# Last feed-forward unit by tile, two residuals on ScalarE and Pool, last output in two stores

## The reference, cut to what matters

```
x = x + xattn(ctx, layernorm(x), mask)
h = silu(q(n) @ q(w_gate).T) * (q(n) @ q(w_up).T)     # n = layernorm(x), 352 columns
x = x + q(h) @ q(w_down).T
```

## Time and profile before

| what | value |
|---|---|
| median of 3 runs | 218.21 us (218.11 to 219.34) |
| profiled execution | 219.57 us, span 217.6 us, so 1.97 us lie outside the span |
| TensorE busy | 187.8 us, 86% |
| VectorE busy | 176.5 us, 81% |
| Pool busy | 139.3 us, 64% |
| ScalarE busy | 131.8 us, 61% |
| granted TensorE clock, mean of the run | 0.973 |

### The profile page before, as it was taken

One profiled execution on the slowest core, in us unless ns is written; L12 is line 12 of the kernel. 1 busy time (PEld: TensorE's weight loads), 2 busy tenths in 40 slices (PEclk: granted clock), 3 DMA queues, 4 the chain that ended last, 5 costly groups with the idle time before them and its releaser, 6 DMA issues.

```text
span 217.6 us, 5689 instructions
## 1 busy us (share of the span) xinstructions
PE 187.8 (86%) x2045; PEld 141.5 (65%) x2045; DVE 176.5 (81%) x391; ACT 131.8 (61%) x264; POOL 139.3 (64%) x203
## 2 busy tenths in 40 slices
PE   0839988979998999998998998796898988899963
PEld 0318574856967769587696775475676766677753
DVE  6417785898799876978769987999999999999941
ACT  2362697957878877798786744364455383665441
POOL 6272737188969592672926577676689875777750
PEclk9985999999999999999999999699999999999998
DMA  6999632040200000000000000000101010101111
GB/s 190 268 293 345 225 115 81 7 144 3 96 3 5 3 0 0 5 3 3 0 3 5 0 5 0 0 0 2 50 3 48 0 48 3 48 2 51 48 49 48
DMA packets 13665, 11.97 MB, mean 55 GB/s; under 512 B 766, under 2 KB 10558, under 8 KB 13630
## 3 DMA queue, kind: packets, MB, share of 16 engines
q1 hardware_dynamic: 13078, 11.29, 16.8%
q10 hardware_dynamic: 560, 0.33, 0.5%
HBM read 9.52 MB, written 2.10 MB: 53 GB/s over the span
## 4 chain that ended last, share of the span: by engine, by line
PE 31%; POOL 20%; issue 14%; DVE 7%; ACT 4%; POOLq 0%; DVEq 0%; ACTq 0%
POOL hq L372 7%; POOL wq_y L357 5%; PE bank L890 4%; PE bank L946 4%; PE bank L949 3%; PE bank L899 3%; PE bank L900 2%; PE bank L878 2%; PE bank L970 2%; POOL xn L254 2%; ACT xn L411 2%; PE a_pair L841 2%; POOL sch L364 2%; PE bank L841 2%; ACT val L423 2%
## 5 line engine op out<-in xcount | busy, mean ns | idle before, releaser
L970 PE MATMUL bank<-wdT,hT 128*128 128x128 f32 x192 | 27.1, 278 | 4.1 <-issue 3.3
L946 PE MATMUL bank<-guT,xqT 128*128 128x352 f32 x64 | 25.5, 481 | 4.3 <-DVE hh L732 4.3
L372 POOL TENSOR_TENSOR hq<-wq_u,sch 128x704 f32<-128x704 f32 x16 | 22.6, 1410 | 9.5 <-DVE wq_u L759 9.4
L970 PEld LDWEIGHTS bank<-wdT,hT 128*128 128x128 f32 x192 | 23.9, 191 | 5.4 <-issue 4.4
L949 PE MATMUL bank<-guT,xqT 128*128 128x352 f32 x64 | 25.0, 473 | 0.0
L357 POOL TENSOR_TENSOR wq_y<-hh,ivh 128x704 f32<-128x704 f32 x16 | 22.5, 1407 | 3.9 <-DVE ivh L747 3.3
L878 PE MATMUL bank<-cT,wsT 128*128 128x512 f32 x32 | 16.9, 655 | 6.5 <-DMA cT<-in_ctxT 6.5
L477 ACT ACTIVATE mask_bc<-bank 128x352 f32<-128x352 f32 x32 | 14.7, 458 | 12.3 <-PE bank L946 12.3
L545 ACT COPY hT<-bank 128x384 f32<-128x384 f32 x32 | 15.2, 476 | 10.2 <-PE bank L958 10.2
L532 ACT ACTIVATE a_pair<-wq_y 128x704 f32<-128x704 f32 x16 | 12.2, 763 | 14.8 <-DVE wq_u L759 14.4
L612 DVE TENSOR_REDUCE den<-prob 128x8 f32<-128x512 f32 x32 | 19.8, 666 | 0.0
(11 more groups left out here) (117 smaller groups left out, 497.2 us busy)
## 6 DMA issues: line engine op xcount, KB each, us to landing
cT<-in_ctxT SPq DMA_DIRECT2D x8, 512.0 KB, 5.2
x_all<-in_x SPq DMA_DIRECT2D x8, 256.0 KB, 5.5
mask_bc<-in_mask_rows SPq DMA_DIRECT2D x8, 256.0 KB, 6.3
out_y<-mask_bc SPq DMA_DIRECT2D x8, 256.0 KB, 2.2
wsT<-in_WsT ACTq DMA_DIRECT2D x1, 256.0 KB, 4.2
w_all<-in_wg SPq DMA_DIRECT2D x1, 176.0 KB
w_all<-in_wu SPq DMA_DIRECT2D x1, 176.0 KB
w_all<-in_wd SPq DMA_DIRECT2D x1, 176.0 KB
```

The lines of the kernel that those rows point to most:

```text
L372: nc.gpsimd.tensor_tensor(hq[i][:, :, 0:I].rearrange("p t (n k) -> p t n k", k=BLK), rh[i][:, :, :].rearrange("p (t n) k -> p t n k", t=2) ...
L946: nc.tensor.matmul(gu_bank[2 * n % 3][:, 0:I], xqT[g % 2][:, t], guT[:, 0, :], start=True, stop=True).then_inc(pe_g, 1)
L970: last = nc.tensor.matmul(d_bank[:, j * P:(j + 1) * P], hT[n % 2][:, c, :], wdT[:, c, :], start=(c == 0), stop=(c == 2))
```

## The change

Unit 15, the last, is handled by tile from the scaled product on. Pool computes `yh` in two instructions (`y_tile`), ScalarE takes the absolute values in two (`abs_tile`), each into a bank of its own that the gate and up products no longer use, and VectorE rounds in four (`round_tile`), and so none of them waits for `ah`. The product with the scale is done by Pool for tile 30 (`hq_first_tile`) and by VectorE for tile 31 (`hq_last_tile`). The groups 5 and 6 (`D_BY_ACT`) are read out of `d_bank` by ScalarE (`down_evac`, a plain copy to `y_out`), and Pool adds `x_all` in place (`residual_sum`), both after `hq_first_tile`. The down products of group 7 go to two other banks, tiles 28 to 30 in one, tile 31 in the other. VectorE adds them to `x_all` in two parts (`residual_last`), three tiles and one, and SyncE stores these as two DMAs. `yo_ok` becomes one semaphore per group.

```diff
+LAST_U = UNITS - 1
+D_BY_ACT = (NG - 3, NG - 2)
...
+        at_bank, last_d = (w1, av_bank), (w0, w0, w0, banks[2])
...
+            def store_last(part, t):
+                sp.wait_ge(yo_ok[NG - 1], part)
+                sp.dma_start(out_tiles[:, NT - TILES + t.start:NT - TILES + t.stop, :],
+                             y_out[1][:, t, :]).then_inc(out_d[1], 16)
...
-            for g in range(NG):
+            for g in range(NG - 1):
                 store(g)
+            store_last(1, slice(0, TILES - 1))
+            store_last(2, slice(TILES - 1, TILES))
...
+            def y_tile(t):
+                pool.wait_ge(ivh_ok, UNITS)
+                pool.wait_ge(h_ok, NT)
+                pool.wait_ge(rh_ok, LAST_U - 1)
+                b = slice(t * NB_H, (t + 1) * NB_H)
+                nc.gpsimd.tensor_tensor(yh[1][:, b, :], hh[1][:, b, :],
+                                        ivh[1][:, b].unsqueeze(2).to_broadcast([P, NB_H, BLK]), ALU.mult).then_inc(yt_ok, 1)
+
+            def hq_first_tile():
+                pool.wait_ge(rt_ok, 1)
+                pool.wait_ge(sch_ok, UNITS)
+                pool.wait_ge(pe_t, t_place["h", NT - 5] + 1)
+                nc.gpsimd.tensor_tensor(hq[1][:, 0, 0:I].rearrange("p (n k) -> p n k", k=BLK), rh[1][:, 0:NB_H, :],
+                                        sch[LAST_U % 4][:, 0:NB_H].unsqueeze(2).to_broadcast([P, NB_H, BLK]),
+                                        ALU.mult).then_inc(hqt_ok[0], 1)
+
+            def residual_sum(g):
+                pool.wait_ge(d_ok, D_BY_ACT.index(g) + 1)
+                ys = y_out[g % 2][:, :, :]
+                nc.gpsimd.tensor_tensor(ys, ys, x_all[:, tiles(g), :], ALU.add).then_inc(yo_ok[g], 1)
...
-                if 0 <= u - 2:
+                if 0 <= u - 2 < LAST_U:
                     hq_unit(u - 2)
...
+                if u < LAST_U:
                     y_unit(u)
+                if u == LAST_U:
+                    y_tile(0)
+                    y_tile(1)
+                if u == UNITS + 1:
+                    hq_first_tile()
+                    residual_sum(D_BY_ACT[0])
+                    residual_sum(D_BY_ACT[1])
...
+            def abs_tile(t):
+                act.wait_ge(yt_ok, t + 1)
+                act.wait_ge(h_ok, NT)
+                nc.scalar.activation(at_bank[t][:, 0:I], yh[1][:, t * NB_H:(t + 1) * NB_H, :].rearrange("p n k -> p (n k)"),
+                                     ACT.Abs, scale=MAGIC).then_inc(at_ok, 1)
+
+            def down_evac(g):
+                act.wait_ge(pe_dn, (g + 1) * TILES)
+                past(act, out_d[g % 2], 16 * (g // 2))
+                nc.scalar.copy(y_out[g % 2][:, :, :].rearrange("p t d -> p (t d)"), d_bank[:, :]).then_inc(d_ok, 1)
+
             for m in range(NT + LAG + 1):
+                if m >= NT and (m - LAG - 1) % TILES == 0 and (m - LAG - 1) // TILES - 1 in D_BY_ACT:
+                    down_evac((m - LAG - 1) // TILES - 1)
...
-                if m % 2 and 0 <= (m - 3) // 2 < UNITS:
+                if m % 2 and 0 <= (m - 3) // 2 < LAST_U:
                     h_abs((m - 3) // 2)
+                if m == 2 * LAST_U + 3:
+                    abs_tile(0)
+                    abs_tile(1)
...
+            def residual_last(t):
+                dve.wait_ge(pe_dn, NT - TILES + t.stop)
+                dve.wait_ge(out_d[1], 16 * (NG // 2 - 1))
+                nc.vector.tensor_tensor(y_out[1][:, t, :],
+                                        last_d[t.start][:, t.start * D:t.stop * D].rearrange("p (t d) -> p t d", d=D),
+                                        x_all[:, NT - TILES + t.start:NT - TILES + t.stop, :],
+                                        ALU.add).then_inc(yo_ok[NG - 1], 1)
+
+            def round_tile(t):
...
+                nc.vector.scalar_tensor_tensor(out=uh[:, t, :], in0=at_bank[t][:, 0:I], scalar=FLOOR * MAGIC,
+                                               in1=yh[1][:, b, :].rearrange("p n k -> p (n k)"),
+                                               op0=ALU.max, op1=ALU.add).then_inc(ut_ok, 1)
...
+                nc.vector.scalar_tensor_tensor(out=rh[1][:, b, :].rearrange("p n k -> p (n k)"), in0=at_bank[t][:, 0:I],
+                                               scalar=FLOOR * MAGIC, in1=uh[:, t, :],
+                                               op0=ALU.max, op1=ALU.subtract).then_inc(rt_ok, 1)
+
+            def hq_last_tile():
...
+                nc.vector.tensor_tensor(hq[1][:, 1, 0:I].rearrange("p (n k) -> p n k", k=BLK), rh[1][:, NB_H:, :],
+                                        sch[LAST_U % 4][:, NB_H:].unsqueeze(2).to_broadcast([P, NB_H, BLK]),
+                                        ALU.mult).then_inc(hqt_ok[1], 1)
 
             for m in range(NT + LAG + 2):
                 if m < NT:
                     h_product(m)
-                if m < NT and (m - LAG) % TILES == 0 and on((m - LAG) // TILES - 1):
+                if (m - LAG) % TILES == 0 and 0 <= (m - LAG) // TILES - 1 < D_BY_ACT[0]:
                     residual((m - LAG) // TILES - 1)
...
+                if m == 2 * LAST_U + 4:
+                    round_tile(0)
+                    round_tile(1)
+                    hq_last_tile()
...
-                if m >= NT and (m - LAG) % TILES == 0 and on((m - LAG) // TILES - 1):
-                    residual((m - LAG) // TILES - 1)
+            residual_last(slice(0, TILES - 1))
+            residual_last(slice(TILES - 1, TILES))
...
             def h_transpose(n):
-                pe.wait_ge(hq_ok, u + 1)
+                if u < LAST_U:
+                    pe.wait_ge(hq_ok, u + 1)
+                else:
+                    pe.wait_ge(hqt_ok[n % 2], 1)
...
             def down(n):
+                bank = d_bank if g < NG - 1 else last_d[j]
+                if n == NT - 1:
+                    pe.wait_ge(rh_ok, LAST_U)
                 if j == 0:
-                    past(pe, yo_ok, g)
+                    if g == NG - 1:
+                        pe.wait_ge(h_ok, NT)
+                    elif g - 1 in D_BY_ACT:
+                        pe.wait_ge(d_ok, 1)
+                    elif g > 0:
+                        pe.wait_ge(yo_ok[g - 1], 1)
```

More of the change, by code:

```diff
@@ L160, in xattn_ffn @@
             sem(n) for n in ("pe_x0", "x0_ok", "pe_t", "t_ok", "pe_g", "pe_u", "pe_dn"))
-        sg_ok, h_ok, amh_ok, uph_ok, ivh_ok, sch_ok, yh_ok, ah_ok, uh_ok, rh_ok, hq_ok, yo_ok = (
+        sg_ok, h_ok, amh_ok, uph_ok, ivh_ok, sch_ok, yh_ok, ah_ok, uh_ok, rh_ok, hq_ok, d_ok = (
             sem(n) for n in ("sg_ok", "h_ok", "amh_ok", "uph_ok", "ivh_ok", "sch_ok", "yh_ok", "ah_ok",
-                             "uh_ok", "rh_ok", "hq_ok", "yo_ok"))
+                             "uh_ok", "rh_ok", "hq_ok", "d_ok"))
+        yt_ok, at_ok, ut_ok, rt_ok = (sem(n) for n in ("yt_ok", "at_ok", "ut_ok", "rt_ok"))
+        hqt_ok = [sem(f"hqt_ok{t}") for t in range(2)]
+        yo_ok = [sem(f"yo_ok{g}") for g in range(NG)]
         x_tiles = x.rearrange("(n p) d -> p n d", p=P)
@@ L193, in store @@
             def store(g):
-                sp.wait_ge(yo_ok, g + 1)
+                sp.wait_ge(yo_ok[g], 1)
                 sp.dma_start(out_tiles[:, tiles(g), :], y_out[g % 2][:, :, :]).then_inc(out_d[g % 2], 16)
+            def store_last(part, t):
+                sp.wait_ge(yo_ok[NG - 1], part)
+                sp.dma_start(out_tiles[:, NT - TILES + t.start:NT - TILES + t.stop, :],
+                             y_out[1][:, t, :]).then_inc(out_d[1], 16)
             load_x(0)
@@ L221, in _ @@
                 load_c(g)
-            for g in range(NG):
+            for g in range(NG - 1):
                 store(g)
-            for s in range(2):
-                sp.wait_ge(out_d[s], 16 * (NG // 2))
+            store_last(1, slice(0, TILES - 1))
+            store_last(2, slice(TILES - 1, TILES))
+            sp.wait_ge(out_d[0], 16 * (NG // 2))
+            sp.wait_ge(out_d[1], 16 * (NG // 2 + 1))
         @block.gpsimd
@@ L775, in _ @@
                     s3_round(NG - 3)
-                if m % 2 == 0 and 0 <= m // 2 - 2 < UNITS:
+                if m % 2 == 0 and 0 <= m // 2 - 2 < LAST_U:
                     h_round(m // 2 - 2)
+                if m == 2 * LAST_U + 4:
+                    round_tile(0)
+                    round_tile(1)
+                    hq_last_tile()
                 if m % 2 and m < NT:
@@ L969, in down @@
                 for c in range(3):
-                    last = nc.tensor.matmul(d_bank[:, j * P:(j + 1) * P], hT[n % 2][:, c, :], wdT[:, c, :],
+                    last = nc.tensor.matmul(bank[:, j * P:(j + 1) * P], hT[n % 2][:, c, :], wdT[:, c, :],
                                             start=(c == 0), stop=(c == 2))
```

11 lines of the change are left out of this document (10 added, 1 removed).

## The result

The changed kernel took **217.50 us** (median of 7, 217.08 to 217.67), the kernel before 218.78 (median of 7, 218.11 to 219.65). The ratio is 0.9935, with a 95% interval of 0.9912 to 0.9959: shorter by 0.65%. That is less than the 1% which the prediction took as the least that can be told from no change. Forecast were 216.3 and a range of 215.8 to 217.0, a gain of 1.89 us. The median missed the range by 0.5 us, and the gain came out 0.5 to 0.6 smaller.

A forecast was written before the change was run, and what follows sets the result against it. No one engine sets the span; in the tail VectorE sets T28. Gains of 0.48 and 0.74 us up to D31's end, then earlier residual and stores, make 1.89 saved: 218.21 - 1.89 = 216.3 us, range 215.8 to 217.0.

The forecast's parts named there:

- the sum's own time: Whole kernel: the 1.89 us saved in the tail, taken off the median of three, 218.21, gives 216.3.
- The residual of group 5: VectorE after product 31: moving this residual to ScalarE and Pool starts tile 28's transposes 0.48 us earlier.
- T28: TensorE's three transposes of tile 28's quantised product: would start at 207.92 us, 0.48 earlier than 208.40.
- The banks: TensorE, down matmuls of tiles 28 to 31: two banks nobody has to empty remove a wait, 0.74 us in all.
- D31's end: End of tile 31's three down matmuls, TensorE's last work: 212.98 us forecast, against 214.20 before.
- ScalarE's copy of group 6: New ScalarE copy before tile 29's down matmuls: just fits, costed at nothing, with 0.1 us as its other end.
- The second store's quarter: Last group's second store: its quarter of the traffic ends before the stream would, so the end is first issue + 2.2 us.
- Rival 1: Last residual: nothing holds it, as Pool's sum goes ahead of VectorE or is nearer 1.06; 2.18 us saved, 216.0, chance 0.2.
- 0.1 to either side: Margin in us kept for the added semaphores, which have no row; the nearest existing waits cost under 0.1 each.
- The split's weight: Unit 15 by tile: makes room for the banks' gain, since tile 30's transposes would otherwise wait until 211.04 us.
- Rival 3: Store of group 5 lands 0.5 us later still, through a slower sum or T28 less early: 216.8, chance 0.12.
- Rivals 2 and 4: 2: last group's second store pays its whole latency, 216.7, chance 0.13; 4: TensorE's clock falls from T28, 221.4, chance 0.04.

The follow-up runs named there:

- a5_unit_whole: Changed kernel with unit 15 handled as a whole again, residuals, banks and stores as changed: span 216.32 us, 14.67 us of it from VectorE's product 31 on.

## Why the prediction was wrong

**The step that failed is the last but one: the sum's own time.** "The terms come from the tail of the profiled one, whose 1.4 above the median I take to lie elsewhere", and then 218.21 - 1.89. It was right that the 1.4 lay elsewhere. But it was the start, and the start is drawn anew in each execution: spans of the unchanged kernel run from 214.2 to 217.8 us, and its tail was 14.94 in both profiles of it. A median of three (218.21) and one of seven (218.78, the three among them) differ by 0.57 with nothing changed, and 0.57 is more than the 0.5 by which the result missed the range. From 218.78 the same sum gives 216.9, and the same range would have ended at 217.6, above the 217.50 measured. The seven executions of the changed kernel had spans of 214.9 to 215.4, so with a tail of 12.76 product 31 came at 202.1 to 202.7, the late end of the 199.2 to 202.7 of all its nineteen executions. When run again the same kernel gave 216.22. "Everything before 203 us keeps its order" is true, and it does not mean that it keeps its time. The range had terms for the unknown costs of the change and none for this, which was readable in the 1.2 us between the three times given.

**The tail was right up to D31.** The residual of group 5: 0.48 forecast, 0.47 measured from product 31 to T28, 0.46 by undoing it. The banks: 0.74 forecast, 0.76 measured from T28 to D31's end, 0.63 by undoing them. T28 at 207.92 and 207.97, D31's end at 212.98 and 213.01, the roundings 0.52 and 0.53, Pool's sum 1.27 and 1.28. ScalarE's copy of group 6 did not delay D29. The second store's quarter hides behind the first one's traffic: 2.2 from the first issue to the landing of the last, 0.57 gained by two stores.

**Rival 1 was the truer one in the span.** I let VectorE's `hq` of tile 31 go first, since it asks 0.06 earlier; Pool's sum went first. It began at 208.61, right behind Pool's tile 30, and VectorE's operation only at 208.69. The last residual was therefore not held, the step to the first issue gained 0.95 and not 0.67, and the tail lost 2.18, rival 1's figure, instead of 1.89. Outside the span 0.25 came back, for which the forecast had no term beyond "0.1 to either side" for the semaphores, and those cost nothing. 2.18 less about 0.2 is 2.0, and over the executions taken together and with the filled start 1.8 to 2.0 of time was measured: near 1.89 because two errors cancel, which is luck.

**The split's weight** was put too low in one respect. The prediction says that it "makes room" for T30, 0.7 by the experiment. It also decides when group 5's store goes out; that is 1.2 more without it. Rival 3 had the mechanism, at 0.5.

**Rivals 2 and 4** did not happen. The last store landed 1.6 us after its own issue, and the granted clock was 1.00 in every stretch of the tail.

## What to carry to other kernels

Measure a change to the tail by a distance inside the trace, from an event ahead of the change to the end of the span; it repeats here to 0.02 us, where the times spread by over 3. Before a forecast is tied to a median of three, look at how far the three lie apart, and give the range that much more. And when TensorE idles for microseconds at the start for a load that only a small side product needs, move that product: here it took the ratio to the kernel before from 0.9915 to 0.9781, about 3 us (2 between the means of all executions, since two of six still started late), where the rework of the tail gained about 2.

## What the runs showed of the hardware that was not expected

The granted clock's record says 1.00 for 0 to 13.6 us, but the first four 512-column matmuls took 3.75 us in the changed kernel with the bias product later and 1.96 with TensorE kept busy from 2.3 us on:

```profile
6.36 3.75 PE L970 MATMUL bank<-cT,wsT 128*128 128x512 f32 x4 [6.36 <-DMA cT<-in_ctxT]
```

```profile
6.30 1.96 PE L970 MATMUL bank<-cT,wsT 128*128 128x512 f32 x4 [0.32 <-DMA cT<-in_ctxT]
```

With one store for the last group the record still says 1.00 where the 16 matmuls from 15.84 on took 3.54, against 1.95 (both lines above). So at the start the durations, not the record, tell which of the two levels TensorE is at. The Trainium skill, "TensorE: Matmul & The Clock Gate", Part 1, says that the throttled level is the default and that activity releases it. The two lines agree: 3.75 us with TensorE idle up to then, 1.96 behind 3.6 us of the added products.

A VectorE operation with two SBUF inputs that asked at about 208.65 waited for a Pool operation that had begun at 208.61, right behind another Pool operation, and took 1.59 instead of 0.53. Pool's second sum, beside the rest of it, took 1.52; in a5_unit_whole, with no such operation beside them, both sums took 1.27. Here the one that had started went first; a lead of a few hundredths in asking is not enough to forecast from.
